# Token numbers placed by matrix products, inverse roots in fewer steps, and a first sequence whose rows go ahead

## What is computed

```python
# layer 0, cross attention: only the softmax itself is added to x
kv = ctx @ W_k.T + b_k
sim = einsum('bid,bjd->bij', einsum('bij,bjd->bid', layernorm(x), kv), kv) * 512 ** -0.5
sim = (sim - mean) * rsqrt(var + EPS) * ln_gamma + ln_beta
x = x + softmax(sim)
# layer 0, feed forward: a dense part and 8 experts, 2 of which each token uses
h = layernorm(x)
dense = rms(gelu(rms(h) @ w_gate) * (rms(h) @ w_up) @ w_down)
top_w, top_i = top_k(softmax(rms(h) * router_scale * ROOT @ router_w), 2)
moe = rms(sum over the two experts of top_w * expert(rms(h)))
x = x + rms(dense + moe)
# layer 1: grouped causal attention with rms norms and rotary tables, then
x = x + (silu(x @ w_gate.T) * (x @ w_up.T)) @ w_down.T
```

## Time and profile before

| | us |
|---|---|
| median of 3 runs | 1894.06 |
| lowest and highest | 1890.92 and 1896.76 |
| the profiled execution, device time | 1889.51 |
| the profiled execution, first to last instruction (span) | 1887.8 |
| PE busy in the span | 1700.5 |
| DVE busy | 1145.1 |
| ACT busy | 797.8 |
| POOL busy | 269.6 |

### The profile page before, as it was taken

The page is one execution under the profiler, slowest core; times in us unless marked ns, Lnnn a source line. Parts: engine busy times, 40 slices in busy tenths (PEclk is TensorE's granted clock), DMA queues, the critical chain, the costliest instruction groups (busy, mean ns, idle before and its releaser), DMA issues. The chain is left out here.

```text
span 1887.8 us, 27233 instructions
## 1 busy us (share of the span) xinstructions
PE 1700.5 (90%) x9396; PEld 1349.7 (71%) x9396; DVE 1145.1 (61%) x2506; ACT 797.8 (42%) x1789; POOL 269.6 (14%) x270
## 2 busy tenths in 40 slices
PE   3688988599988999787999999978999999999998
PEld 3576876488887987665767667766776678678887
DVE  6798777255665745984566766689646563553222
ACT  4465553143665753322555555433245452431111
POOL 1224126523121203220000000222100000000000
PEclk8699988799999999998999999988989999999999
DMA  3325567389789887779335316988873445236562
GB/s 108 107 101 179 167 195 270 121 317 346 252 271 328 279 306 295 241 274 303 94 118 158 106 46 202 383 297 317 270 235 105 125 123 204 77 125 209 186 219 97
DMA packets 127063, 384.93 MB, mean 204 GB/s; under 512 B 15680, under 2 KB 30416, under 8 KB 121168
## 3 DMA queue, kind: packets, MB, share of 16 engines
q1 hardware_dynamic: 119088, 360.61, 56.6%
q0 software_dynamic: 7840, 22.59, 3.5%
HBM read 278.78 MB, written 104.37 MB: 203 GB/s over the span
## 5 line engine op out<-in xcount | busy, mean ns | idle before, releaser
L1185 PE MATMUL ps<-xT,gu 128*128 128x512 f32 (+1 forms) x1392 | 535.0, 384 | 78.5 <-DVE act L1662 31.7
L1187 PE MATMUL ps<-xT,gu 128*128 128x512 f32 (+1 forms) x1392 | 514.5, 370 | 4.0 <-issue 4.0
L1186 PE MATMUL ps<-xT,gu 128*128 128x512 f32 (+1 forms) x1392 | 514.3, 369 | 4.1 <-issue 4.1
L1185 PEld LDWEIGHTS ps<-xT,gu 128*128 128x128 f32 x1392 | 271.3, 195 | 131.8 <-issue 39.2
L1187 PEld LDWEIGHTS ps<-xT,gu 128*128 128x128 f32 x1392 | 270.0, 194 | 49.0 <-issue 5.6
L1186 PEld LDWEIGHTS ps<-xT,gu 128*128 128x128 f32 x1392 | 270.9, 195 | 40.9 <-issue 4.8
L1185 PE MATMUL ps<-wd,hid 128*128 128x512 f32 x604 | 248.9, 412 | 28.3 <-DVE acc L1697 13.9
L1186 PE MATMUL ps<-wd,hid 128*128 128x512 f32 x604 | 239.3, 396 | 0.0
L1187 PE MATMUL ps<-wd,hid 128*128 128x512 f32 x604 | 239.0, 396 | 0.0
L1390 ACT ACTIVATE hid<-act 128x512 fp32r<-128x512 f32 (+1 forms) x174 | 100.0, 575 | 281.0 <-DVE act L1662 278.2
L1662 DVE TENSOR_TENSOR act<-act,ps 128x512 f32<-128x512 f32 (+1 forms) x174 | 106.8, 614 | 157.7 <-PE ps L1187 150.8
(11 more groups left out here) (277 smaller groups left out, 2282.5 us busy)
## 6 DMA issues: line engine op xcount, KB each, us to landing
gu<-w_dram SPq DMA_DIRECT2D x160, 512.0 KB
raw<-in_ffn_w SPq DMA_DIRECT2D x94, 768.0 KB
wd<-w_dram SPq DMA_DIRECT2D x80, 512.0 KB, 5.6
w_dram<-gu SPq DMA_DIRECT2D x32, 1024.0 KB
w_dram<-wd SPq DMA_DIRECT2D x32, 512.0 KB
QT<-q_dram SPq DMA_DIRECT2D x48, 256.0 KB, 4.9
y_dram<-x SPq DMA_DIRECT2D x23, 512.0 KB
wcs<-tab_dram SPq DMA_DIRECT2D x16, 512.0 KB, 5.9
```

Source lines behind the costliest of these rows:

```text
L1185: mm(out_ap, ah, bh, start=start, stop=False)
L1186: mm(out_ap, ah, bl, start=False, stop=False)
L1187: return mm(out_ap, al, bh, start=False, stop=stop)
```

## The change

Four edits.

1. The scatter goes. For each of 16 token tiles, DVE now writes four small tables of marks (`hot`): for each expert choice k, a 128x128 table that is 1 where the lane number equals the slot's low seven bits (`lane_hot`), and a 128x46 table that holds the token's number where the column equals the slot's tile (`tile_hot`). PE multiplies the two (`spot`, two matmuls of 128x46 per token tile) and sums all 32 products in bank 5. One copy on DVE (`rowno`) turns the sum into `row_of`. `zero`, the 32 indirect transfers and `tokload` are gone.
2. The inverse root takes one Newton step and one third-order step on a scaled number. The twelve small instructions of a root become nine, and `simstats` loses one more, since its factor now lies in the scaling. There are 41 such roots. `ROOT` is 3 pieces instead of 4.
3. `held_behind` in the planner: the splits of weight tiles 0 and 1 may not be placed ahead of `bet(0, 3)`, `rn2` not ahead of `sim(0, 3)`, `ctx(1)` not ahead of `resid(0, 3)`, `stats1(1, 0)` not ahead of the end of `stats2(0)`.
4. Prices of the roots in the planner, and the prices of the new steps.

```diff
-    ROOT = 4
+    ROOT = 3
...
-        return ticks + [[("scatter", n)] for n in range(NT // 2)] + [[("tokload",)]]
+        return ticks + [[item] for t in range(NT) for item in (("hot", t), ("spot", t))] + [[("rowno",)]]
...
-            return [("DVE", 1.4 if a[-1] == 0 else 0.7)]
+            return [("DVE", (1.0, 0.7, 1.1 if kind == "qnorm" else 0.85)[a[-1]])]
...
-            "scatter": lambda: [("slots", 1), ("zero", 0)], "tokload": lambda: [("scatter", n) for n in range(NT // 2)],
-            "xs": lambda: [("tokload",)] + [("x1store", n) for n in range(B)] + [("xstore", B - 1, n) for n in range(TB)] if b < 2 else [("xgt", b - 2, RB - 1)],
+            "hot": lambda: [("slots", 1)] + [("spot", b - 2)] * (b > 1), "spot": lambda: [("hot", b)], "rowno": lambda: [("spot", NT - 1)],
+            "xs": lambda: [("rowno",)] + [("x1store", n) for n in range(B)] + [("xstore", B - 1, n) for n in range(TB)] if b < 2 else [("xgt", b - 2, RB - 1)],
...
+    def held_behind(item):
+
+        if item[0] == "w" and item[1] < 2:
+            return [("bet", 0, TB - 1)]
+        return {("rn2",): [("sim", 0, TB - 1)], ("ctx", 1): [("resid", 0, TB - 1)], ("stats1", 1, 0): [("stats2", 0, TB + ROOT - 1)]}.get(item, [])
...
-                    for t in (2 * n, 2 * n + 1):
-                        for k in range(2):
-                            nc.gpsimd.indirect_dma_start(row_dram, bass.IndirectOffsetOnAxis(ap=place[:, k, t:t + 1], axis=0), tokens[:, t:t + 1], None).then_inc(rows_placed, 16)
...
+                elif kind == "spot":
+                    t = a[0]
+                    pe.wait_ge(hot_ready, t + 1)
+                    for k in range(2):
+                        last = mm(ps[:, 5, 0:NB * RB], lane_hot[:, t % 2, k, :], tile_hot[:, t % 2, k, :], start=(t, k) == (0, 0), stop=(t, k) == (NT - 1, 1))
+                    last.then_inc(spotted, 1)
...
-                    link(V_.tensor_scalar(y.bitcast(I32), z.bitcast(I32), -1.0, 1597463007.0, ALU.mult, ALU.add))
-                    link(V_.tensor_scalar(v, v, -0.5, None, ALU.mult), True)
+                    link(V_.tensor_scalar(y.bitcast(I32), z.bitcast(I32), -1.0, 1597463007.0 + 1073741824.0, ALU.mult, ALU.add), True)
+                    return
+                link(tt(out=z, in0=y, in1=y, op=ALU.mult))
+                link(tt(out=z, in0=z, in1=v, op=ALU.mult))
+                if step == 1:
+                    link(stt(out=y, in0=z, scalar=3.0, in1=y, op0=ALU.add, op1=ALU.mult), True)
                 else:
-                    link(tt(out=z, in0=y, in1=y, op=ALU.mult))
-                    link(tt(out=z, in0=z, in1=v, op=ALU.mult))
-                    link(stt(out=dst if step == ROOT - 1 else y, in0=z, scalar=1.5, in1=y, op0=ALU.add, op1=ALU.mult), True)
+                    link(stt(out=z, in0=z, scalar=40.0 / 3.0, in1=z, op0=ALU.add, op1=ALU.mult))
+                    link(stt(out=dst, in0=z, scalar=80.0, in1=y, op0=ALU.add, op1=ALU.mult), True)
...
+                elif kind == "hot":
+
+                    t = a[0]
+                    settled()
...
+                    if t > 1:
+                        dve.wait_ge(spotted, t - 1)
+                    for k in range(2):
+                        V_.tensor_scalar(lane_hot[:, t % 2, k, :], lanes[:, :], lane_of[:, k, t:t + 1], None, ALU.is_equal)
+                        last = V_.tensor_scalar(tile_hot[:, t % 2, k, :], lanes[:, 0:NB * RB], tile_of[:, k, t:t + 1], tokens[:, t:t + 1], ALU.is_equal, ALU.mult)
+                    last.then_inc(hot_ready, 1)
+                elif kind == "rowno":
+                    dve.wait_ge(spotted, NT)
+                    V_.tensor_copy(row_of[:, :], ps[:, 5, 0:NB * RB]).then_inc(free[5], 1)
```

More of the change, by code:

```diff
@@ L271, in steps @@
             "xt": [("POOL", 1.0), ("ACT", 0.53), ("DVE", 0.6)], "top2": [("DVE", 1.4)], "weights": [("ACT", 0.33), ("DVE", 1.2)], "ranks": [("PE", 0.36), ("DVE", 0.4)],
-            "before": [("DVE", 1.1)], "blocks": [("DVE", 1.2)], "places": [("DVE", 1.1)], "slots": [("DVE", 1.0)], "scatter": [("POOL", 5.1)], "xs": [("POOL", 2.55)],
+            "before": [("DVE", 1.1)], "blocks": [("DVE", 1.2)], "places": [("DVE", 1.1)], "slots": [("DVE", 1.0)], "hot": [("DVE", 0.65)], "spot": [("PE", 0.42)], "rowno": [("DVE", 0.15)], "xs": [("POOL", 2.55)],
             "xgt": [("PE", 0.36), ("ACT", 0.48), ("DVE", 0.6)], "kprep": [("POOL", 4.2 if a and a[0] == 0 else 5.0 if a and a[0] > B else 4.4)], "wo": [("ACT", 0.95), ("DVE", 1.15)], "ksq": [("ACT", 1.0)],
@@ L277, in steps @@
             "split": [("ACT", 0.53), ("DVE", 0.6)], "project": [("PE", 2.85), ("DVE", 0.6)], "rown4": [("ACT", 0.71)], "rowt4": [("PE", 0.36), ("ACT", 0.48), ("DVE", 0.6)],
-            "rn2": [("DVE", 1.5), ("PE", 2.0), ("ACT", 0.5)], "zero": [("POOL", 0.75)]}.get(kind, [])
+            "rn2": [("DVE", 1.5), ("PE", 2.0), ("ACT", 0.5)]}.get(kind, [])
     def builds_on(item):
@@ L386, in banks @@
             return (4,)
-        if kind in ("kvturn", "ranks"):
+        if kind in ("kvturn", "ranks") or (kind, *a) == ("spot", 0):
             return (5,)
@@ L410, in leaves_bank @@
         return {"sim": ("scale", *a), "scores": ("exp", *a), "values": ("norm", *a[0:2]), "gate0": ("gate" if mode(a[0]) == "table" else "mix", a[0]) if kind == "gate0" else None,
-                "up0": ("mult", *a), "downs": ("down", *a[0:2])}.get(kind, item)
+                "up0": ("mult", *a), "downs": ("down", *a[0:2]), "spot": ("rowno",)}.get(kind, item)
     def merge(streams):
@@ L428, in ready @@
             for item in tick:
-                on = [o for o in builds_on(item) if o not in inside and min(o[1:], default=0) >= 0]
+                on = [o for o in builds_on(item) + held_behind(item) if o not in inside and min(o[1:], default=0) >= 0]
                 if any(o not in end for o in on):
@@ L539, in two_layers @@
     SIDES[-B].insert(3, [("rn2",)])
-    SIDES += [[[("zero", 0)]], routing_ticks(), key_ticks()]
+    SIDES += [routing_ticks(), key_ticks()]
     for pair in range(0, B, 2):
@@ L643, in two_layers @@
         m1, m2, pk = (sb("r_" + n, [P, NT], F32, a_scope) for n in ("m1", "m2", "pk"))
-        no_rows, tokens = sb("no_rows", [P, NB * RB], I32, a_scope), sb("tokens", [P, NT], I32, a_scope)
-        slot_q, slot_p = sb("slot_q", [P, 2, NT], I32, a_scope), sb("slot_p", [P, 2, NT], F32, a_scope)
-        place = sb("place", [P, 2, NT], mybir.dt.uint32, a_scope)
+        tokens, lanes = sb("tokens", [P, NT], F32, a_scope), sb("lanes", [P, P], F32, a_scope)
+        tile_i = sb("tile_i", [P, 2, NT], I32, a_scope)
+        tile_of, lane_of = (sb(n, [P, 2, NT], F32, a_scope) for n in ("tile_of", "lane_of"))
+        lane_hot = sb("lane_hot", [P, 2, 2, P], F32, a_scope)
+        tile_hot = sb("tile_hot", [P, 2, 2, NB * RB], F32, a_scope)
         a2_scope = ExitStack()
@@ L946, in _ @@
                             load(out[b, rows(t), :], x[:, b % 2, t, :]).then_inc(out_stored, 16)
-                elif kind == "tokload":
-                    sp.wait_ge(rows_placed, 16 * 2 * NT)
-                    load(row_of[:, :], row_dram.rearrange("(p n) o -> p (n o)", p=P).bitcast(mybir.dt.uint32)).then_inc(row_of_loaded, 16)
                 elif kind == "kstore":
@@ L1112, in _ @@
                     if k == 0:
[L1113 removed]
+                        pool.wait_ge(free[5], use(5, "spot", 0))
                         pool.wait_ge(x1_stored, 16 * B)
```

47 lines of the change are left out of this document (19 added, 28 removed).

## The result

The changed kernel took 1863.05 us (median of 4 executions, 1861.5 to 1864.6), against 1895.41 us for the kernel before beside it (4 executions, 1890.9 to 1899.9). The ratio is 0.9829, with a 95% interval from 0.9803 to 0.9855: 32 us faster. The forecast was 1864.5 us.

What follows compares the result with a forecast made beforehand. PE was taken as the bound, busy 1700.5 of 1887.8 us, so gains come from its idle or lower-clock time. Terms -24 +7.6 +2 +1 -7 -2 -7 = -29.4 gave 1864.5 us against 1894.06; eight-in-ten range 1847 to 1884.

Steps and rivals of the forecast that it cites:

- the stall: Part 1, 331 to 362 us: scatters hold up what feeds the engines; removing them gives -24 us, bounds 0 and -26.
- marks: Part 2, routing: +7.6 us of PE products, +2 of PE waiting for DVE, +1 for gathers.
- roots: Part 3: shorter inverse roots relieve DVE, -7 us in the norm stretches and -2 from 85 to 315 us.
- holding back: Part 4, kernel start: first sequence goes ahead, first main tile 14.5 us earlier; worth -7 us, bounds -12 and -2.
- parts 2 to 4 together: Whole kernel without the stall's term: marks, shorter roots and head start, -5.4 us in all.
- second sign: Around the scatters: the instruction queue moved only two packets in 65 us, read with tiny writes holding up the engines' feed.
- The first rival: 331 to 362 us: the stall has another cause and stays; 1888.5 us, within 0.3% of before; chance 0.08.
- all of it lies on PE, the bound: Routing: the 32 marks' matmuls, 7 to 10 us, count in full on PE, +7.6 us.
- the forecast's mechanism: Norm stretches, 760 to 840 and 1200 to 1320 us: 14.4 us less DVE work fills PE's 36 us idle; half taken, -7.
- Its first half: Chain before the first main tile: first norm 1.8 us earlier than 16.9 us, `scale` at 35.7 instead of 39.4 us.
- DVE has the same work as before still to do: Up to 315 us: DVE, nearly full, limits the 14.5 us earlier start, so only -7 us was taken.
- -7 for the norms: Norm stretches before the attention: half of the roots' 14.4 us of DVE relief, bounds -14 and +6.

Runs made afterwards that it cites:

- e6: The kernel after, unchanged, run again in a later set beside the kernel before: 1860.16 us, ratio 0.9938.
- e1: The kernel before with the marks alone in place of the scatters, old roots, nothing held back: 1883.81 us, ratio 1.0082.
- e7: The kernel before with the three-step inverse root alone: 1858.20 us, ratio 0.9936.
- e4: The kernel before with the holding back of sequence 1's rows alone: 1869.23 us, ratio 0.9994.
- e5: The kernel before, unchanged, run and traced again in a later set: 1868.88 us.
- e11: The kernel after with both sets of marks in fp32r instead of f32: 1868.50 us, ratio 0.9849.
- e9: The kernel after with the 32 four-byte-row scatters added behind POOL's eighth gather, written to a tensor nobody reads: 1863.09 us, ratio 0.9951.
- e12: The kernel after with 24 scatters of four-byte rows, then 24 of 512-byte rows, added behind POOL's eighth gather: 1863.47 us, ratio 0.9967.
- e8: The kernel after with the 32 scatters of before added ahead of POOL's first gather, to a tensor nobody reads: 1875.68 us, ratio 1.0035.
- e2: The kernel after without the holding back of sequence 1's rows: 1859.76 us, ratio 0.9957.
- e3: The kernel after with the old four-step inverse root: 1884.86 us, ratio 1.0087.
- e10: The kernel after with the marks made on POOL instead of DVE: 1894.14 us, ratio 1.0133.

## Why the prediction was right, and where it was not

The total was right, 1864.5 against 1863.05 us, and the largest term, the stall, was sized rightly. The sum was not right term by term, and that it came out within 1.5 us is luck twice over: misses cancel, and the comparison fell into a set with the stall. In e6's set the same change is worth 8.7 us by the medians, against the 29.6 forecast. For the three edits, the ratio less one times the median of before in the same set gives each part:

```
term                       forecast   measured (95%)
stall, removed                -24     about -24 by the times of before: two sets of six
marks                         +10.6   +15.3 (+9.9 to +21.0), e1
roots                          -9     -12.0 (-15.5 to -8.4), e7
holding back                   -7     -1.1 (-3.6 to +1.1), e4
parts 2 to 4 together          -5.4   -11.6 (-15.9 to -7.1), e6
```

**The stall (part 1).** Its size was read rightly: 22.4 us of lost matmuls and 2 us at the lower clock, 24 in all, and the same kernel without it is 24 to 27 us shorter. What the forecast did not see is that it belongs to some sets of runs only; three executions of one set could not tell. And its second sign, the two packets of the instruction queue, is no sign, since e5 has the same two. The first rival, that the stall has another cause and stays, has lost in the two slow sets: neither after nor e11, which have no scatter, shows it. In the four other sets the Trainium skill's rule ("DMA: Bandwidth & Descriptors", section "Queues, rings and completion order": queues served in turn, instruction refill on a row of queues kept for the runtime) fits what is seen in e5, e9 and e12: scatters in flight and nobody held up. That the scatters themselves make the stall is argued, not shown. It coincides with them in the only trace that has it, and it is absent from two kernels of such sets that lack them. But those two differ from before in more than the scatters, and none of the runs with scatters added or moved (e8, e9, e12) came to lie in a set with the stall. What differs between sets, on one and the same chip, stays open too.

**The marks (part 2).** The instructions were priced well: the products are 8.7 us of PE against 7.6, a group of four comparisons takes 0.82 us of DVE (two pairs 0.41 us apart) against an estimate of 0.78, the wait is 1.3 us against 2, and the gathers cost 0 against 1. But what they cost at the place is another thing: from tile 18 to 36, e1 and e6 both lose only 3.8 us to e5. From 315 to 480 us PE is idle 5.2 us in e5 and 1.9 us in e6 (first e5, then e6), so part of the work went into gaps:

```profile
315.00:480.00 165.00, 159.78 (x839) 136.24 (x838) 93.63 (x150) 70.44 (x136) 67.30 (x63) 1.00 0.86 305
```

```profile
315.00:480.00 165.00, 163.10 (x879) 140.13 (x879) 102.67 (x201) 69.79 (x133) 34.39 (x27) 1.00 0.85 298
```

This is the step that failed in the first set as well, "all of it lies on PE, the bound": forecast -13.4 from tile 18 to 36, measured -21.7, and 6.8 us of that miss are the marks (10.6 forecast, 3.8 by e6). The remaining cost of the marks alone comes elsewhere: in e1 nothing of the marks stands behind tile 24, yet it lies 7.4 us behind e5 at tile 36, 12.9 at tile 120 and 15.6 at the end. (At tile 96 it is 28.0, but there e7, which has no marks, is 21.7 behind as well.)

**The roots (part 3).** -12.0 against -9, inside the bounds, but not by the forecast's mechanism: it had PE's idle time shrink, and in e7 that is as long as in e5 while PE is busy 10.0 us less. Beside the marks they are worth more, by e2 and e1 23 us (ratio of the ratios 0.9876). The forecast had bounds for such interplay of the plan (-14 to +6) and took the middle; alone the middle was right.

**The head start (part 4).** This is the term that was most mis-sized for its size: -7 against -1. Its first half came as written: the first norm at 14.3 (15.1 forecast) and `scale` at 35.68 (35.7). Then the second norm came at 58.56 instead of 55.5. The forecast took `rn2` out of the first norm and put its price nowhere; it now stands here and takes DVE 3.35 us, from 39.77 to 43.12. The four products of `yT` alone, its first part, took 2.69 us where they took 0.87 in before:

```profile
L1703 DVE TENSOR_SCALAR yT<-ident,rnp x4: 273/678/1300, 39.8 to 42.2; 128x128 f32<-128x128 f32 x4
```

Two of them started while POOL's `va` products ran (36.61 to 41.99) and took 1.08 and 1.30 us; they ended 0.09 and 0.08 us behind the end of a POOL instruction. The two behind POOL's last took 0.27 us each. By the Trainium skill's rule of the port pair that DVE and POOL share, held for a whole instruction ("SBUF — State Buffer", section "SBUF: two separate sides"), the one that comes second waits; the trace agrees. From the norm to the first main matmul it then took 20.7 us and not 15. Behind the first transposed row PE waits 3.8 us in all for DVE and ACT, and the four transposes of sequence 1 between the rows are 1.1 us; the rest of the 5.7 is not traced. Third, what was put off had to be done all the same: `pkv` and `sim` inside the first tile, the first nine main matmuls at the lower clock, and DVE still busy 182 of the 230 us behind the start. Of the 5.8 us at the first main matmul nothing was left at the first product in the first set, 1.4 in e6 against e5 and 2.0 in e4. The passage of the forecast that "DVE has the same work as before still to do" was the right argument; it spoke for the near bound, -2.

**The sum.** In the first set three misses cancel. Ahead of tile 18 the forecast had -9 and +5.8 came, 14.8 us too hopeful, of which 5 may be chance by the caution above; from tile 18 to 36 it had -13.4 and -21.7 came; behind it -7 for the norms and -12.3 came. Without the stall, e6 against e5, the three are -0.5, +3.8 and -11.2. The forecast's own range, 1852 to 1876, is also narrower than the bounds of its terms added up, which give 1849 to 1894 even with the stall's term kept at -24. The parts do not add up either: alone they make +2.2 us (15.3 - 12.0 - 1.1), together -11.6. Nearly 14 us of gain, give or take 8 by the intervals, lie in how the planner fits them together, and I have found no instruction to which they belong. The table of tiles shows only where: between tiles 36 and 120 the kernels with marks and old roots lose 5.5 and 7.1 us to e5 (e1, e3), the others of the table gain 1.3 to 8.8. The pages show in what form. PE's busy and idle time against e5, one trace each:

```
                     PE busy   PE idle
e1 marks alone          +2.8     +14.4
e7 roots alone         -10.0      +0.4
e4 holding back         -9.5      +9.2
e6 the whole change     -0.2      -7.7
```

Two traces of the kernel after (first set and e6) differ by 4.8 us busy and 2.3 idle. So the marks alone cost waiting, where the forecast had them as work on PE, and it is this waiting that is gone when all parts are together; holding back gains on PE's busy time what it loses in waits. I could not tell why. No version was shown better than the kernel after: e7 equals it where there is no stall, has the scatters, and was not run where there is one; e2, e9, e11 and e12 are within the intervals of after or above it.

## What to carry to other kernels

A second set of runs tells more than further executions in the first: an odd stall in one trace may be a property of the set, and a change that removes it is then worth 24 us or nothing, as here. Price work put into a stretch against the gaps that this stretch has. Work moved behind the first tile has to be done all the same: where the engine that must do it was already about 80% busy, as DVE here, an earlier start was worth next to nothing. When an instruction is moved, add its price where it lands. Where a planner lays out the whole kernel anew, measure the parts of a change together too; here, alone, they added up to 14 us less gain than together.

## What the runs showed of the hardware that I had not expected

The same program on the same chip took 1894 to 1900 us in all nine executions of one set and 1863 to 1875 in all thirteen of the next. In the one trace of the slower kind, from 331 to 362 us, all transfers fall to 23 GB/s, DVE and ACT are busy 3.1 and 0.5 us and PE 13.45 of 31 while 32 transfers of 128 four-byte rows are under way; in the second kind 32 such transfers (e5, e9), or 24 and then 24 of 512-byte rows (e12), pass beside 250 to 390 GB/s of traffic with PE busy 29.5 of 31 us or more. On PE, a product of 128x46 in fp32r is one record with a median of 268 ns, in f32 two overlapping records with a median of 287 ns (e11 and after, the rows above). A comparison of 128x128 with a scalar per row takes 283 ns on DVE and about 600 ns on POOL, as rows of e10 in order of time show:

```profile
345.44 0.62 POOL L1111 TENSOR_SCALAR lane_hot<-lanes,lane_of 128x128 f32<-128x128 f32 x1
346.02 0.55 POOL L1112 TENSOR_SCALAR tile_hot<-lanes,tile_of,tokens 128x46 f32<-128x46 f32 x1
```
